# Products that nobody reads, added to TensorE's queue in each update of a recurrence

## The reference, cut to what matters

```python
def step(carry, xs):
    cp, cm = carry
    k_t, v_t, q_t, a_t, th_t, e_t = xs
    g = jax.vmap(jax.grad(loss_fn))(cp, k_t, v_t)
    s = lambda c: c[:, :, None]
    nm = jax.tree_util.tree_map(lambda m, gg: m * s(e_t) - s(th_t) * gg, cm, g)
    np_ = jax.tree_util.tree_map(lambda p, m: p * (1.0 - s(a_t)) + m, cp, nm)
    out_t = jax.vmap(_mlp, in_axes=(0, 0))(np_, q_t)
```

## Time and profile before

| | |
|---|---|
| time, median of 3 runs | 10934.41 us (10927.46 to 10938.42) |
| the profiled execution's own time | 10920.32 us |
| its span, first to last instruction | 10918.5 us |
| PE busy | 9048.3 us, 83% |
| DVE busy | 4914.1 us, 45% |
| ACT busy | 2119.8 us, 19% |
| POOL busy | 227.6 us, 2% |
| mean granted clock of TensorE | 0.855 of full |

### The profile page before, as it was taken

One profiled execution on the slowest core, in us unless ns is written; L12 is line 12 of the kernel. 1 busy time (PEld: TensorE's weight loads), 2 busy tenths in 40 slices (PEclk: granted clock), 3 DMA queues, 4 the chain that ended last, 5 costly groups with the idle time before them and its releaser, 6 DMA issues. The chain is left out here.

```text
span 10918.5 us, 371322 instructions
## 1 busy us (share of the span) xinstructions
PE 9048.3 (83%) x151474; PEld 5910.9 (54%) x151474; DVE 4914.1 (45%) x13031; ACT 2119.8 (19%) x4839; POOL 227.6 (2%) x184
## 2 busy tenths in 40 slices
PE   6799944325699999999999999999999999967777
PEld 2466621123466676666666666667667666642222
DVE  3444435447444434434344444443443444445555
ACT  0233312221111111111111111111111111113433
POOL 0000000001100000000000000000000000000000
PEclk8799965558698898898988988989889898888888
DMA  2000001426211111211121111222222222200000
GB/s 61 8 11 11 11 24 40 136 43 133 52 33 52 54 56 52 57 52 54 53 56 53 55 54 55 76 73 82 68 74 81 68 77 77 59 21 12 11 9 11
DMA packets 961784, 563.10 MB, mean 52 GB/s; under 512 B 376334, under 2 KB 956694, under 8 KB 959766
## 3 DMA queue, kind: packets, MB, share of 16 engines
q1 hardware_dynamic: 947990, 544.62, 18.4%
q0 software_dynamic: 13312, 12.57, 0.6%
HBM read 331.63 MB, written 188.08 MB: 48 GB/s over the span
## 5 line engine op out<-in xcount | busy, mean ns | idle before, releaser
L2373 PE MATMUL bank<-mv,hdiag 128*32 128x144 f32 x63744 | 2085.9, 289 | 9.5 <-DVE hdiag L2565 8.9
L2373 PEld LDWEIGHTS bank<-mv,hdiag 128*32 128x32 f32 x63744 | 1956.8, 111 | 94.7 <-DVE hdiag L2565 13.1
L2426 PE MATMUL bank<-mvt,ydiag 128*32 128x256 f32 x31872 | 1944.3, 381 | 0.1
L2426 PEld LDWEIGHTS bank<-mvt,ydiag 128*32 128x32 f32 x31872 | 1038.6, 110 | 570.0 <-issue 3.2
L2300 PE MATMUL bank<-hist,hdiag 32*128 32x256 f32 x2048 | 499.0, 669 | 217.3 <-DVE hdiag L2510 217.3
L2243 ACT ACTIVATE work<-work 128x128 f32<-128x128 f32 x498 | 154.3, 310 | 2219.7 <-DVE work L2555 2219.7
L431 PE MATMUL att_bank<-att_qa,att_ka 32*124 32x248 f32 x2048 | 580.3, 410 | 0.5 <-DVE att_qa L645 0.5
L421 PE MATMUL att_bank<-att_ka,att_qn 32*124 32x496 f32 x1024 | 574.2, 658 | 3.7 <-DVE att_mx L606 3.7
L606 DVE TENSOR_REDUCE att_mx<-att_bank 124x2 f32<-124x496 f32 x512 | 344.7, 674 | 486.6 <-PE att_bank L421 486.6
L2598 DVE TENSOR_TENSOR rep<-bank,ta 128x128 f32<-128x128 f32 x249 | 72.7, 292 | 1029.4 <-PE bank L2373 1029.4
L2313 PE MATMUL bank<-r_ident,mvt 128*128 128x128 f32 x2048 | 502.9, 427 | 39.3 <-DVE mvt L2528 39.3
(11 more groups left out here) (414 smaller groups left out, 10927.0 us busy)
## 6 DMA issues: line engine op xcount, KB each, us to landing
ring<-between_slopes SPq DMA_DIRECT2D x320, 512.0 KB, 4.1
baset<-between_base_old SPq DMA_DIRECT2D x265, 128.0 KB, 2.0
baset<-between_base SPq DMA_DIRECT2D x265, 128.0 KB, 2.2
between_base<-work SPq DMA_DIRECT2D x256, 128.0 KB
hist<-h SPq DMA_DIRECT2D x1992, 8.0 KB
hist<-y SPq DMA_DIRECT2D x1992, 2.0 KB
hist<-dl SPq DMA_DIRECT2D x1992, 8.0 KB
between_base_old<-bo SPq DMA_DIRECT2D x240, 128.0 KB
```

Source lines behind the costliest of these rows:

```text
L2373: mm = e.matmul(psP[32 * j:32 * j + 32, 0:MW], hdiag[:, hf, r, j, :], mv1[:, hf, r, j, :], start=(hf == 0 and r == 0), stop=(hf == 1 and r ...
L2426: mm = e.matmul(psBack[hf][32 * j:32 * j + 32, :], ydiag[:, n, j, :], both, start=(n == 0), stop=(n == 7))
```

## The change

A helper issues f32 products of a 128x128 identity with the 512 columns of `yth` into a bank that is free at the time. Nobody reads the results. There are 16 before `new_terms(0)`, as soon as DVE and ACT have ended the chunk before; one into each of `psC[0]` and `psC[1]` at the start of every `turned(X)`, where the wait for ACT's copies of the slab before is taken ahead of the wait for DVE; 3 before L2356, after ACT's last copy of the update; 4 between L2356 and the first transpose of step 0. That is 55 an update, 880 in all.

```diff
+                    def kept_warm(out, n):
+
+                        for _ in range(n):
+                            e.matmul(out, ident[:, :], yth[:, :, :].rearrange("p a s -> p (a s)"), start=True, stop=True)
+
...
                     def turned(X):
                         for k in range(2):
+                            if X:
+                                e.wait_ge(A.sem, A.upd(c, f"c{X - 1}{k}1"))
+                            kept_warm(psC[k], 1)
+                        for k in range(2):
                             j, m, g, n = slab(X, k)
                             e.wait_ge(V.sem, V.upd(c, f"sn{X}{k}"))
-                            if X:
-                                e.wait_ge(A.sem, A.upd(c, f"c{X - 1}{k}1"))
...
+                    e.wait_ge(V.sem, V.begun(c))
+                    e.wait_ge(A.sem, A.begun(c))
+                    settled(e, s_pe)
+                    kept_warm(psC[0], 16)
                     new_terms(0)
                     new_terms(1)
...
                     mm.then_inc(T.sem, 1)
+                    e.wait_ge(A.sem, A.upd(c, "c1511"))
+                    kept_warm(psC[0], 3)
                     e.wait_ge(V.sem, V.upd(c, "d3c"))
...
+                    kept_warm(psC[0], 4)
                     e.wait_ge(T.sem, T.upd(c, "cb"))
```

## The result

The changed kernel takes 11000.93 us (median of 5 runs, 10980.41 to 11003.66) against 10935.6 for the kernel before in the same job (5 runs, 10927.46 to 10948.7): a ratio of 1.0052, 95% interval 1.0039 to 1.0066. It is slower by 0.5%, where I had forecast 0.3% faster. The profiled execution took 11003.66 us and its span is 11001.9; its mean granted clock rose from 0.855 to 0.914.

A forecast was written before the change was run, and what follows sets the result against it. TensorE at its lower clock level was taken to bound the updates. Head +6.3, slabs -8.6, tail +1.95, step 0 -2.3 gave -2.65 us a middle update, -36 in all: 10,898 us, range 10,845 to 10,950 (8 in 10).

The forecast's parts named there:

- The tail's step: Between slabs and step 0: three and four products delay L2356 and the first transpose; +1.95 us an update.
- The slabs' term: Slab pipeline: clock rises to 2.4 GHz, rounds take 7.78 or 8.6 us; -8.6 us an update.
- rival C: Level up, but head and slabs cancel: +3.6 us an update at worst, 10,915 to 10,990 us; chance 0.20.
- The head: Start of the update: 16 products take 13.7 us and delay VectorE's slab chain; +6.3 us for a middle update.
- rival B: Slabs: the clock level does not rise; some 70 us an update more, 12,050 us; chance 0.05.
- the weight load: Added products: each instruction's weight load lies under the product before and costs nothing.
- rival D: Added products: weight load of each instruction not hidden, 0.21 us; net +19 us an update, 11,240 us; chance 0.07.
- the first products: Start of step 0: the first sum takes 8.6 us instead of 10.94; -2.3 us an update.
- The lower bound of the slabs' term: Slab pipeline with 0.93 us a product and 1.89 for L2338: 4.4 us gained an update.
- the reading: Old slab stretch: TensorE busy 66.78 of 72.33 us, no idle over 1 us between groups, yet clock 0.50.

The follow-up runs named there:

- e1_no15: The changed kernel without the two products at the start of turned(15), the other 53 kept; 10967.1 us, ratio 1.0044.
- e8_trim: The changed kernel with one product per X up to 13, none for 14 and 15, 8 at the head, 1 and 2 in the tail; 10730.2 us, 0.9824.
- e10_fill: e8_trim with SP issuing the base stores first, plus two products in the gap before the second round; 10611.7 us, ratio 0.9718.
- e3_rows32: The changed kernel with all 55 products of an update using 32 rows instead of 128; 11794.2 us, one run.
- e11_gap_order: e6_gap with SP issuing the base stores first; 10552.8 us, ratio 0.9662.
- e6_gap: The changed kernel with slab products moved from turned() to TensorE's waits before new_terms of even X, 8 at the head, 1 and 2 in the tail; 10828.7 us, 0.9918.
- e5_slab_only: The changed kernel without the 16, 3 and 4 products of head and tail, only the slab products kept; 10863.1 us, ratio 0.9950.
- e7_one: The changed kernel with one product in turned(X) instead of two, into psC[0] only; 10819.2 us, one run.
- e4_no_slab: The changed kernel without any product in turned(), those of head and tail kept; 11074.9 us, one run.

## Why the prediction was wrong

The forecast's sum over 16 updates was -36 us; the parts measured give +49, that is +3.0 an update against -2.3. The miss of 5.3 us an update is the tail's 2.5, the slabs' 2.2 and the head's 0.5.

- **The tail's step failed.** I had written that the products' wait for ScalarE's copies costs nothing, "ScalarE's copies, for which the products now wait in place of the transposes, are done before VectorE's slab is", and for the tail I counted only the three and the four products, from 1.7 us after the slabs. For the last X there is no `new_terms` left ahead of the products: they wait for ScalarE's copies of X = 14, which end 1.10 us after the last slab and not before it, start 0.60 us after the slab and put 1.82 us before its transposes (3788.76 to 3790.58). ScalarE's last copy ends later by that, and the three products, which wait for it, begin 4.3 us after the slabs (3792.48) instead of 1.7. L2369 comes at 7.0 us instead of 4.35, L2372 at 11.1 instead of 8.45, L2386 at 11.96 instead of 9.4. From there on the forecast's distances hold; all is 2.6 us late. e1_no15 shows 1.16 of it as the two products of X = 15; the rest is the wait for the copies of X = 14, as the rows of the last transposes show (1.23 us after the slabs' end in e1_no15 by that wait, 0.34 before it in e8_trim without it). e8_trim differs in other counts too, and no run takes out the products of X = 14 alone.
- **The slabs' term was right at the higher level and too large in the mean.** Third update 64.5 us where I said near 64, round with L2345 8.7 where I said 8.6, plain 7.86 against 7.78, and by the chain foreseen: one half of 4.01 us, in which TensorE goes on as soon as VectorE has the next right-hand side, and one of 3.85 of its own work. The mean, 66.2, holds the falls of the clock in the second round: six updates with 1.7 us and four with 3.2 are 1.4 an update, which the forecast put at nothing and I had only as a part of rival C and at the head alone. Two products in the gap before it keep the clock at 1.00 (e10_fill). The rest, some 0.8, is that the third update gains 7.85 us (72.33 to 64.48) and not 8.6.
- **The head** is +7.4 in the mean, against 6.3 for a middle update (6.9 with the first and the last). Third update: start 0.77 us after POOL's, as foreseen, 0.87 a product instead of 0.85; in some updates the gap ahead of it has the clock down and the 16 take 15.6 us.
- **Right:** the level rises (rival B is out, and e3_rows32 shows what it would look like); the weight load is hidden (0.87 a product; rival D is out); the first products take 8.6 us; between the updates all stays but for 0.6 us a chunk. Rival C had the direction, a cancelling with the clock down in a gap; its "worst" of +3.6 us an update is near the measured +3.0 by luck, as it has the slabs at -4.4 (-6.6 measured) and the tail at +1.95 (+4.5).
- **Two slips without weight.** The lower bound of the slabs' term, -4.4, adds up to about -3.6 by its own figures, since a round with L2338 then gains nothing. And the old slab stretch did have idle times over 1 us between groups, 2.13 and 1.11 us ahead of its first transposes and its second round; from there on the reading holds.
- **What my argument did not ask:** whether the products of one place are needed for the level of the next. Fewer of them, off the path, and SP's order changed, give -2.8 to -3.4% (e10_fill, e11_gap_order); without the change to SP it is -0.8% in the gaps alone (e6_gap) and -1.8% in e8_trim.

What stays open: why the start of the first update moves by up to 28 us between profiled executions of unchanged earlier stages, why one gap of 1.99 us lowers the clock and the same gap in the update before does not, and what brings the level up in one update of e3_rows32 and not in the next.

## What to carry to other kernels

Work that holds the clock up must stand where the engine would wait anyway: behind the wait for another engine's result and in no larger amount than that wait. In front of an instruction on the path, or behind a third engine's buffer at the end of a pipeline where nothing else covers it, a product costs up to its full time: 55 an update made this kernel 0.5% slower, 21 in the gaps alone made it 0.8% faster, and 3.4% with SP's queue in another order. When one stage gets faster, read the queues beside it again: SP's order of transfers, free in the kernel before, lengthened one round already where rounds of 8.7 us came without a longer head (e5_slab_only), and was the bound at 6.5.

## What the runs showed of the hardware

- TensorE busy 60.00 of 60.00 us with 32-row products between its transposes stayed at a granted clock of 0.50 (e3_rows32, fourth update). The slab windows of that kernel have 0.50 to 0.71, with 34 us at 1.00 in the eighth update; with 128-row products in the same places they have 0.95 to 1.00 (the change). In the slab stretch of e7_one one product for each X held 0.94 to 0.97; the same stretch without any went back to half speed in its second round (e4_no_slab).
- The higher level, once lost, did not come back with one product for two X: after its wait of 8.13 us e6_gap ran on at the durations of 1.2 GHz, a group of eight L2306 in 2.08 us, with TensorE busy all but that wait (third update, 3702.61 to 3727.78). It came back behind the first place with two products (L2306 in 1.13 us at 3731.33). The same products hold a level that is up (e11_gap_order, 0.94 to 1.00).
- Ahead of the second round of the changed kernel stands a gap of 1.99 or 2.00 us in 14 updates, 2.33 and 2.38 in two. The clock fell in 9 of the 14 and in one of the two, and stayed up in the other six.
